# A score mask written into PSUM by ScalarE instead of by mask products, with head-by-head score banks and query transposes moved

## The reference

```python
# 16 heads of 64, windows of 32 tokens; every query sees its own window and the one before it
bk2, bv2 = (look(bk), look(bv))                       # 64 keys for each window
mask = (it < jb) | (it > jb + w) | (jb == -1)
sim = jnp.einsum('bhwie,bhwje->bhwij', bq, bk2) * QK_SCALE
sim = jnp.where(mask, -jnp.finfo(sim.dtype).max, sim)
attn = jax.nn.softmax(sim, -1)
out = jnp.einsum('bhwij,bhwje->bhwie', attn, bv2)
```

## Time and profile before

| | |
|---|---|
| runs | 3923.66, 3922.48, 3933.7 us; median 3923.66 |
| profiled execution | 3917.23 us, span 3915.3 us |
| granted TensorE clock, mean | 0.960 of full speed |
| TensorE (PE) busy | 3590.0 us, 92% of the span |
| VectorE (DVE), ScalarE (ACT), GpSimd (POOL) busy | 73%, 62%, 59% |

### The profile page before, as it was taken

How to read it: one execution, slowest core, us unless ns; L and a number is a source line. 1 busy time by engine, 2 the same in 40 slices (tenths; PEclk the granted TensorE clock), 3 DMA queues, 4 the chain that set the end, 5 groups by cost and what they waited for, 6 DMA issues and landing times.

```text
span 3915.3 us, 129350 instructions
## 1 busy us (share of the span) xinstructions
PE 3590.0 (92%) x51660; PEld 1831.4 (47%) x51660; DVE 2866.5 (73%) x6058; ACT 2413.5 (62%) x4153; POOL 2295.5 (59%) x2171
## 2 busy tenths in 40 slices
PE   3799999999999999999676899999999999999997
PEld 2354444444544444544343454544445444444543
DVE  1788778778778778786325878778778777877874
ACT  2467766756766766766312567666666666666674
POOL 0767656666666666665002766666666666666661
PEclk6899999999999999999777999999999999999999
DMA  5000000000000000000000001001001001001000
GB/s 176 10 14 23 20 15 21 21 15 21 21 15 21 21 15 21 21 11 18 34 0 3 10 14 32 13 13 33 11 13 33 11 13 33 11 15 32 12 5 12
DMA packets 50170, 83.76 MB, mean 21 GB/s; under 512 B 7168, under 2 KB 37120, under 8 KB 47232
## 3 DMA queue, kind: packets, MB, share of 16 engines
q1 hardware_dynamic: 49536, 75.05, 6.1%
HBM read 67.69 MB, written 7.34 MB: 19 GB/s over the span
## 4 chain that ended last, share of the span: by engine, by line
PE 83%; issue 10%; ACT 3%; DVE 2%; POOL 1%; DMA 1%; SPq 0%; DVEq 0%; ACTq 0%; POOLq 0%
PE VS L870 19%; PE QA L810 18%; PE TB L829 9%; PE TB L894 9%; PE VS L917 7%; PE TB L853 5%; PE FB L943 3%; PE FB L952 3%; PE FB L944 3%; PE VS L908 2%; ACT KT L448 2%; PE TB L837 1%; PE FB L928 1%; PE FB L933 1%; DMA KT<-in_w_out 1%
## 5 line engine op out<-in xcount | busy, mean ns | idle before, releaser
L330 POOL TENSOR_TENSOR QN<-T 128x512 f32<-128x512 f32 x768 | 980.1, 1276 | 679.7 <-DVE T L596 503.4
L337 POOL TENSOR_TENSOR QN<-QN,RR 128x512 f32<-128x512 f32 x768 | 800.6, 1043 | 392.1 <-DVE RR L617 392.1
L810 PE MATMUL QA<-WQ,Y 128*128 128x512 f32 x1536 | 845.5, 634 | 59.3 <-DVE T L596 20.2
L870 PE MATMUL VS<-MW,Y 128*32 128x512 f32 x6144 | 816.3, 605 | 1.7 <-DVE Z L669 1.7
L591 DVE TENSOR_TENSOR T<-QA,TAB 128x512 f32<-128x512 f32 x768 | 525.2, 684 | 114.4 <-ACT SQ L434 98.2
L454 ACT ACTIVATE V<-VS 128x512 f32<-128x512 f32 x768 | 458.5, 598 | 233.4 <-PE VS L870 232.5
L434 ACT ACTIVATE SQ<-QA 128x512 f32<-128x512 f32 x768 | 459.9, 599 | 198.9 <-PE QA L810 172.9
L596 DVE TENSOR_TENSOR T<-QA,TAB 128x256 f32<-128x256 f32 x1536 | 571.7, 413 | 4.2 <-issue 4.2
L894 PEld LDWEIGHTS TB<-CST,QN 128*128 128x128 f32 x3072 | 355.0, 142 | 394.1 <-issue 351.2
L894 PE MATMUL TB<-CST,QN 128*128 128x128 f32 x3072 | 488.6, 282 | 15.4 <-POOL QN L337 15.4
L604 DVE TENSOR_REDUCE SSQ<-SQ 128x8 f32<-128x512 f32 x768 | 487.9, 676 | 0.0
(11 more groups left out here) (154 smaller groups left out, 4175.3 us busy)
## 6 DMA issues: line engine op xcount, KB each, us to landing
TAB<-in_tables SPq DMA_DIRECT2D x192, 128.0 KB, 2.1
WQ<-in_w_qk SPq DMA_DIRECT2D x48, 256.0 KB, 3.1
MW<-m_dram SPq DMA_DIRECT2D x12, 1024.0 KB, 4.8
m_dram<-QN SPq DMA_DIRECT2D x6, 1024.0 KB, 4.9
W1R<-in_w SPq DMA_DIRECT2D x12, 341.0 KB, 3.1
KT<-in_w_vt SPq DMA_DIRECT2D x6, 512.0 KB, 5.8
KT<-in_w_out SPq DMA_DIRECT2D x6, 512.0 KB, 6.6
W<-in_w SPq DMA_DIRECT2D x12, 192.0 KB, 2.4
```

The lines of the kernel that those rows point to most:

```text
L330: po.tensor_tensor(QN[:, n % 2, k, :], T1[:, k, :], T2[:, k, :], ALU.add).then_inc(s_add, 1)
L337: po.tensor_tensor(heads(QN[:, m % 2, k, :]), heads(QN[:, m % 2, k, :]), RR[:, m % 2, 8 * k:8 * k + 8].unsqueeze(2).to_broadcast([P, 8, DH ...
L810: mm(QA[:, k % 2, :], Y[:, j * P:(j + 1) * P], WQ[:, k, :], start=True, stop=True).then_inc(s_qk, 1)
L870: last = mm(VS[32 * q:32 * q + 32, w % 2, :], Y[:, a:a + WIN], MW[:, q, :], start=True, stop=True, tile_position=(0, 32 * q), skip_group_c ...
```

## The change

ScalarE writes the fp32 mask, one 64-column pattern per partition repeated for 16 heads, into both score banks (`mask_seed`), ahead of `qk_out(2, 3)`; the score products then all run with `start=False`. The banks are laid out head by head, so one product writes 64 adjacent columns, and VectorE takes the maximum in one instruction. `qk_transpose(1, 2)` moves ahead of the up products and the scores. The identity IDB and its DMA go. The mask is still loaded by one DMA, now in fp32.

```diff
+        def both(bank):
+            return bank[:, :, :].rearrange("p e (c k) -> p (e c) k", k=2 * WIN)
...
+                def mask_seed():
+                    m = n - 2
+                    after(ac, s_z, 1, n - 3, 0, it, s)
+                    after(ac, s_ve, 4, n - 4, 3, it, s)
+                    nc.scalar.activation(both(VS), MASKN[:, 0 if m % TPL == 0 else 1, :].unsqueeze(1)
+                                         .to_broadcast([P, HEADS, 2 * WIN]), ACT.Copy).then_inc(s_seed, 1)
...
                 if live(c, 0, it):
                     square(3)
                 if live(c, 2, it):
+                    mask_seed()
                     qk_out(2, 3)
...
+                    nc.vector.tensor_reduce(MX[:, m % 2, :], both(VS), AX.X, ALU.max).then_inc(s_mx, 1)
+                    ve.wait_ge(s_mx, by_tile(1, m, it, 1))
                     for e in range(2):
-                        nc.vector.tensor_reduce(MX[:, m % 2, e, :], VS[:, e, :].rearrange(
-                            "p (a c k) -> p c a k", a=2, c=CH), AX.XY, ALU.max).then_inc(s_mx, 1)
-                    for e in range(2):
-                        ve.wait_ge(s_mx, by_tile(2, m, it, e + 1))
                         ins = nc.vector.tensor_tensor(
-                            Z[:, m % 2, e * GT:(e + 1) * GT].rearrange("p (a c k) -> p a c k", a=2, c=CH),
-                            VS[:, e, :].rearrange("p (a c k) -> p a c k", a=2, c=CH),
-                            MX[:, m % 2, e, :].unsqueeze(1).unsqueeze(3).to_broadcast([P, 2, CH, WIN]), ALU.subtract)
+                            Z[:, m % 2, e * GT:(e + 1) * GT].rearrange("p (a c k) -> p c a k", a=2, c=CH),
+                            VS[:, e, :].rearrange("p (c a k) -> p c a k", a=2, c=CH),
+                            MX[:, m % 2, CH * e:CH * e + CH].unsqueeze(2).unsqueeze(3).to_broadcast([P, CH, 2, WIN]),
+                            ALU.subtract)
...
-                    if edge:
-                        after(pe, s_z, 1, n - 3, 0, it, s)
-                    after(pe, s_ve, 4, n - 4, 3, it, s)
                     pe.wait_ge(s_te3, by_tile(1, m, it, 1))
-                    for e in range(2):
-                        mm(VS[:, e, :].rearrange("p (a c k) -> p a c k", a=2, c=CH), IDB[:, :],
-                           MASKN[:, 0 if m % TPL == 0 else 1, :, :].unsqueeze(2).to_broadcast([P, 2, CH, WIN]),
-                           start=True, stop=False, skip_group_check=True)
+                    pe.wait_ge(s_seed, by_tile(1, m, it, 1))
+                    pe.sem_inc(s_sc, 1)
...
-                                last = mm(bank[32 * w:32 * w + 32, :, ch, :], QT[r, m % 2, ch, w * WIN:(w + 1) * WIN],
-                                          KT[r, ch, a:a + 2 * WIN].rearrange("p (a k) -> p a k", a=2), start=False,
+                                last = mm(VS[32 * w:32 * w + 32, e, ch * 2 * WIN:(ch + 1) * 2 * WIN],
+                                          QT[r, m % 2, ch, w * WIN:(w + 1) * WIN], KT[r, ch, a:a + 2 * WIN], start=False,
...
                 if live(c, 2, it):
                     qk_transpose(2, 3)
+                if live(c, 1, it):
+                    qk_transpose(1, 2)
                 if up0_g is not None:
                     ffn_up(up0_g, 0)
                 if up1_g is not None:
                     ffn_up(up1_g, 1)
                 if live(c, 2, it):
                     scores()
-                if live(c, 1, it):
-                    qk_transpose(1, 2)
                 if live(c, 3, it):
                     p_transpose(3, 0)
```

More of the change, by code:

```diff
@@ L52, in after, with build_macaron @@
     need(engine, sem, by_tile(per, m, it, k + 1))
-def build_macaron(nc, x, w_qk, w_vt, w_out, q_rows, w1, w2, prm_ffn, w_ret, gn, tables, consts, mask_n, ident,
+def build_macaron(nc, x, w_qk, w_vt, w_out, q_rows, w1, w2, prm_ffn, w_ret, gn, tables, consts, mask_n,
                   dec_a, dec_v, m_dram, out):
-    fp32, bf16 = mybir.dt.float32, mybir.dt.bfloat16
+    fp32 = mybir.dt.float32
     ACT, ALU, AX = mybir.ActivationFunctionType, mybir.AluOpType, mybir.AxisListType
@@ L105, in build_macaron @@
         RR = sb("RR", [P, 2, 32])
-        MX = sb("MX", [P, 2, 2, CH])
+        MX = sb("MX", [P, 2, HEADS])
         SM = sb("SM", [P, 2, 2, CH])
         RC = sb("RC", [P, 2, 2, CH])
-        MASKN = sb("MASKN", [P, 2, 2, WIN], bf16)
-        IDB = sb("IDB", [P, P], bf16)
+        MASKN = sb("MASKN", [P, 2, 2 * WIN])
         CST = sb("CST", [P, 3, P])
@@ L153, in build_macaron @@
         s_xn, s_h, s_y, s_prb, s_w1 = sem("s_xn"), sem("s_h"), sem("s_y"), sem("s_prb"), sem("s_w1")
-        s_sq, s_ve, s_te, s_te3, s_pe, s_ex, s_oe = (
-            sem(n) for n in ("s_sq", "s_ve", "s_te", "s_te3", "s_pe", "s_ex", "s_oe"))
+        s_sq, s_ve, s_te, s_te3, s_pe, s_ex, s_oe, s_seed = (
+            sem(n) for n in ("s_sq", "s_ve", "s_te", "s_te3", "s_pe", "s_ex", "s_oe", "s_seed"))
+        s_sc = sem("s_sc")
         s_rl, s_re, s_fsq, s_fl, s_frs, s_ge = (sem(n) for n in
@@ L206, in _ @@
             sp.dma_start(CST[:, :, :], consts[:, 0:3, :]).then_inc(s_c_in, 16)
-            sp.dma_start(MASKN[:, :, :, :], mask_n).then_inc(s_c_in, 16)
-            sp.dma_start(IDB[:, :], ident).then_inc(s_c_in, 16)
+            sp.dma_start(MASKN[:, :, :], mask_n).then_inc(s_c_in, 16)
             def fold_in(l):
@@ L1023, in stack @@
                 all_slots(pe, slot, s)
-            pe.wait_ge(s_c_in, 16 * 3)
+            pe.wait_ge(s_c_in, 16 * 2)
             pe.wait_ge(s_x_in, 16)
@@ L1130, in shape_constants @@
     rq = np.arange(P) % WIN
[L1131 to L1134, removed]
+    mask_n = np.zeros((P, 2, 2 * WIN), f32)
+    mask_n[:, :, 0:WIN] = np.where(rq[:, None] <= np.arange(WIN)[None, :], 0, big)[:, None, :]
+    mask_n[:, :, WIN:] = np.where(rq[:, None] >= np.arange(WIN)[None, :], 0, big)[:, None, :]
+    mask_n[0:WIN, 0, 0:WIN] = big
     gam = (f32(1.0) - np.exp(np.linspace(np.log(1.0 / 32.0), np.log(1.0 / 512.0), RH)).astype(f32)).astype(np.float64)
@@ L1143, in shape_constants @@
     dec_v = np.concatenate([dq[:, None, :], dk[:, None, :], hm], axis=1).astype(f32)
-    return tables, consts, mask_n, eye, dec_a, dec_v, (gch ** P).astype(f32)
+    return tables, consts, mask_n, dec_a, dec_v, (gch ** P).astype(f32)
 def kernel(**inputs):
     import numpy as np
-    import ml_dtypes
     import concourse.bacc as bacc
@@ L1154 @@
     a = {k: np.ascontiguousarray(v) for k, v in inputs.items()}
-    tables, consts, mask_n, eye, dec_a, dec_v, gch = shape_constants()
-    bf = ml_dtypes.bfloat16
+    tables, consts, mask_n, dec_a, dec_v, gch = shape_constants()
     wqkv = a["L0_ffn_Wqkv"]
@@ L1179 @@
     arrays = dict(x=a["L0_attn_x"], w_qk=w_qk, w_vt=w_vt, w_out=w_out, q_rows=q_rows, w1=a["L0_ffn_W1"], w2=w2,
-                  prm_ffn=prm_ffn, w_ret=w_ret, gn=gn, tables=tables, consts=consts, mask_n=mask_n.astype(bf),
-                  ident=eye.astype(bf), dec_a=dec_a, dec_v=dec_v)
+                  prm_ffn=prm_ffn, w_ret=w_ret, gn=gn, tables=tables, consts=consts, mask_n=mask_n,
+                  dec_a=dec_a, dec_v=dec_v)
     arrays = {k: np.ascontiguousarray(v) for k, v in arrays.items()}
```

1 line of the change is left out of this document (removed).

## The result

The changed kernel takes 3937.9 us (median of 16 runs, 3927.0 to 3968.4), the kernel before in the same rounds 3922.6 (16 runs, 3912.2 to 3940.7): a ratio of 1.0039, 95% interval 1.0021 to 1.0056. It is slower by 0.4%. The forecast was 3840, and the range ended at 3893. The profiled execution takes 3929.6 with a span of 3927.8, 12.5 more than the span of before (3915.3).

The account below looks back on a forecast made before the run. TensorE, busy 92% of the span, was taken as the bound. Slot savings summed to 83 us, taking the profiled 3917.2 to 3834 and the median 3923.7 to 3841, given as 3840, range 3795 to 3893.

Parts of the forecast that it names:

- Mask products: Removed from TensorE ahead of the scores: net 0.45 us saved in centre and down slots, 0.43 in up slots.
- move: Query transposes ahead of the scores fill TensorE's wait: 0.44 us saved in centre and down slots, nothing in up slots.
- seed: ScalarE's mask copy into PSUM before the KT copy: 0.95 us, hidden in down slots, 0.15 late in centre slots.
- attend: Probability-value products after first-up slots wait for a later QT copy: 0.22 us lost instead of 0.43 gained.
- Maximum and subtraction: VectorE's single reduction over both banks and permuted write of Z: same elements, costed at nothing.
- unbroken runs: Score products writing one run of 64 values: worth between 0 and 0.47 us per slot, taken as 0.
- rival 4: Scores speed up to the rate of unbroken runs: 90 us more saved, 3750; chance 0.05.
- The increment: Semaphore increment on TensorE before the scores: 0.14 us charged from KT copy to first score, upper bound about 0.3.
- Rival 2: The increment drains TensorE before the scores: about 40 us lost, 3880; chance 0.15.
- The sum: Savings per slot kind added over the score slots of both stacks: 83 us, forecast given as 3840.
- The range: Whole-kernel time from a little under 3803 to a little over 3880: 3795 to 3893 us.

Follow-up runs that it names:

- move_only: The kernel before with its query transposes put in front of the mask products, nothing else changed: 3881.1 us, ratio 0.9883.
- split_wait: The changed kernel with the KT copy's wait on the last query transpose, moved directly before the scores, instead of on a semaphore increment: 3856.0 us, ratio 0.9812.
- before_shift128: The kernel before with 128 empty semaphore increments ahead of TensorE's first wait: 3943.7 us, ratio 1.0043.
- before_shift214: The kernel before with 214 empty semaphore increments spread over waits for weights in TensorE's opening: 3932.1 us, ratio 1.0021.
- before_inc: The kernel before with an empty semaphore increment, carrying the wait for the KT copy, in front of the mask products: 3978.0 us, ratio 1.0120.

## Why the prediction was wrong

**The bound, and where time could go: right.** TensorE sets the time throughout, and each slot kind changed as its own waits said.

**Mask products, move, seed, attend: right to 0.02 us a slot.** The seed was taken at 0.95 of ScalarE's time; its rows in the changed kernel, in ScalarE's timeline of a first-up slot, answer to the earlier trace rows:

```profile
1057.71 0.60 ACT L436 ACTIVATE SQ<-QA 128x512 f32<-128x512 f32 x1 [0.43 <-PE QA L819]
1058.20 1.02 ACT L469 ACTIVATE VS<-MASKN 128x1024 f32<-128x1024 f32 x1
1059.15 0.59 ACT L450 ACTIVATE KT<-TB 128x512 f32<-128x512 f32 x1
```

The KT copy starts 0.95 after the seed. What is left of the wait for it, forecast at 0.2 to 0.3, is 0.34 in the down and 0.48 in the centre slot above, but the slots as wholes came out as priced. The new wait of attend for the QT copy, 0.58 in this slot, was forecast at about 0.6, and its sum at some 30 us above 3.8; it is 28.4. move_only confirmed the move alone (42.8 for 40).

**Maximum and subtraction at nothing: right.** The subtraction releases project_v with 3.7 us of idle in all, 1.7 before.

**No gain from unbroken runs: right.** A score takes 225 ns, 228 before, and the group 1.47 to 1.48 in the timeline, 1.48 to 1.49 before. The rule of the Trainium skill (PSUM — Partial Sum Buffer, Specifications), by which non-contiguous access patterns slow matmuls significantly, brought nothing here: by it the scores would have become shorter, and rival 4 falls.

**The increment: the step that failed.** The prediction saw it ("the change adds a semaphore increment on TensorE's queue, which this trace does not show") and charged 0.14 a slot, with a full drain of 0.3 as the upper bound. That priced the increment by what it does to products next to it, and there 0.14 is exact (1020.60 to 1020.74 in the chain). It did not ask what else the wait holds up: here the reading ahead of TensorE's own instructions. Rival 2, the increment as a drain at 40 us, named the right instruction with the wrong mechanism and less than half the size; in clean up slots there is no gap before the scores. Without the increment the forecast's terms hold: split_wait takes 3856.0, and the forecast's 3840 with 90 times 0.17 to 0.18 for the transpose behind the wait makes some 3856.

**The sum** therefore lacked a term. Idle of the kind "issue" in and behind the scores is 75.9 us instead of 7.0, 69 more. The clock records of the two loops add up to 102 us at the lower level instead of 55; at most half of that difference, 24, is lost time. With the 80 saved in the slots that gives +13, and the spans differ by 12.5. The second term goes with the stalls: move_only and split_wait, with none or next to none in their scores, spend 41 and 55 us of their loops at the lower clock. Gaps of 3 to 5 us at the end of a loop iteration, eight in all, are in both kernels (30 and 32 us in total) and explain nothing.

**The range** took its ends from prices of rows that were in the trace. The case that came true, a stream of instructions that arrives too late, has no row; but the page of before already listed the queue q8 with 430 pieces of 16 KB, and 256 instructions in 1.42 us could have been set beside it.

What stays open: what exactly makes the sequencer ask for a piece. With a waiting increment some slots get it in time at the same edge (in the changed kernel the centre slot with an edge 229 on stalls in three of ten iterations, the one with 233 in nine of ten), and in kernels without one a few slots of the loops stall all the same (two in the kernel before, five in before_shift128, three in before_shift214, by 1.0 to 1.4 us).

## What to carry to other kernels

A wait that must stand in front of a dense run of small products belongs on a product, not on a semaphore increment of its own: the engine reads ahead past a product that waits, and here it did not read ahead past an increment that waits. Where 256 instructions pass faster than a piece of instructions arrives (1.42 against some 3.5 us from the request here), look at the instruction queue beside the engine's timeline: gaps put down to no semaphore, at distances that are multiples of 256 instructions, are its mark, and moving all instructions by a known number of places shows it. When the price of an added instruction is unknown, adding it alone to the kernel before is the cheapest test there is: before_inc would have shown these stalls, if at half the size.

## What the runs showed of the hardware

- TensorE's sequencer was 4.0 us ahead of the products when nothing held it (increment at 804.4, mask products at 808.44), and a product that waited did not hold it (L929 at 803.7, L871 in front of it at 804.34).
- A piece of 16 KB starts about 1.1 us after the waiting increment is through (1039.1 to 1040.18; 819.6 to 820.76; 0.9 to 1.8 over 186 stalls), and TensorE goes on 2.2 to 3.0 us after that (1042.63; 823.66).
- Behind 2.0 us without a product the granted clock was 0.56 from 1042.90 to 1046.30, and 0.95 in the stretch behind that; two products that take 1.02 took 1.92 and 1.84.
- ScalarE writes 128x1024 values of a broadcast source into two PSUM banks in 1.02 us, no longer than the 1.05 of an exponential of that size in SBUF.
